# Softmax denominators of an attention block: one group an iteration instead of two, y stored before it is divided, gates kept in DRAM

## The chip, the cores and the metric

The kernel runs on 1 core of a Trainium2 chip. The metric is the device time of one execution in microseconds, the median over several runs. Engines are called by the profile's names: PE (TensorE), DVE (VectorE), ACT (ScalarE), POOL (GpSimd), SP (SyncE, which here only issues DMAs).

## The reference

One transformer block with adaptive layer norm, batch B = 2, sequence S = 2048, width H = 512, 16 heads of 32, all float32:

```
c6 = silu(c) @ Wc + bc
sh_msa, sc_msa, g_msa, sh_mlp, sc_mlp, g_mlp = split(c6, 6)
xm = layernorm(x) * (1 + sc_msa) + sh_msa
q, k, v = xm @ Wq + bq, xm @ Wk + bk, xm @ Wv + bv     # 16 heads of 32
w = softmax(q k^T / 32) ; y = w v
x = x + g_msa * (y @ Wo + bo)
xm2 = layernorm(x) * (1 + sc_mlp) + sh_mlp
x = x + g_mlp * (gelu(xm2 @ W1 + b1) @ W2 + b2)
```

## The kernel before

The program has three stages, `project`, `attend` and `feed_forward`, each a block in which every engine runs its own list of instructions, ordered by semaphores alone. At the end of a stage the engines meet.

**project** computes q, k, v and the modulation vectors for 8 blocks of 512 tokens and stores q, k and v in DRAM. It also computes the gates (g_msa, g_msa*bo, g_mlp, g_mlp*b2 for both batch entries, 8 tiles of 128x512), which stay in SBUF in `sh.gates`, 16 KB of each partition.

**attend** has 32 iterations (`N_IT`): iteration i handles one group of 4 heads and 512 queries against all 2048 keys; four iterations (`BPB`) share a head group. In an iteration there are 16 tiles of 128 keys. For each tile and head PE makes scores (L1221), ACT takes their exponential into `probs` (L1054), a ring of 5 tiles, and PE multiplies with v into `y_bank` (L1232), two tiles at a time. Between these PE makes the scores once more for the maxima of the next iteration (L1205), which DVE reduces (L1078).

The denominators are sums of the exponentials over all keys. They are made so:

- Each group of 4 tiles is a quad c (4 an iteration, `QPI`). POOL adds tiles 0 and 1 of the quad (`first_pair`, L905, two instructions, heads 0-1 and 2-3) and tiles 2 and 3 (`second_pair`, L916, two instructions).
- POOL then issues accumulating DMAs (`accumulate`, L920), 1 MB each: `fold_quad` adds the second sum to the first, `fold_half` adds the first sum of an odd quad to that of the even quad before it. Two quads make a half h, so an iteration has 4 quad folds and 2 half folds.
- PE multiplies each half with a matrix of ones (`sums`, L1238), 4 matmuls of 128x32 on 512 columns, which the profile shows as 8 records; when such a group is due says `due_sums`. ACT copies the result (`take_sum`, L991), a small DMA gathers it (`move_sums`), DVE adds the two halves and inverts (`invert_small`), and two more DMAs store the inverses and load them back broadcast over 128 partitions (`store_inv`, `load_inv`).
- ACT copies y out of PSUM (`take_y`), POOL multiplies it with the inverses two iterations later (`normalise`, L954), and ACT's queue stores it to `y_cols` (`store_y`).

A slot of `probs` is given back to ACT only when its y matmuls and POOL's sum over it are done (`slot_free`); a home of a half sum is given back to POOL when PE's `sums` over it is done (`first_free`); `second_pair(c)` waits for the fold of quad c - 2, `fold_half` for that of the odd quad.

The last iteration differs: its sums aren't folded by DMA, DVE makes some of them, and the first output projection, residual, norm and up product of the next stage are worked in.

**feed_forward** runs over 8 blocks k of 512 tokens. A block has 16 steps j (`MT`): PE makes `up(k, j)` and `down(k, j-1)`, each with three products of rounded high and low parts (lines 1677 to 1679, 12 matmuls each); ACT makes gelu (L1655); DVE rounds and splits h (L1552, L1554) and W1, W2 (L1542, L1547), POOL makes their low parts (L1465, L1470). The attention output of block k + 1 is loaded into `yb`, biased by ACT (`bias_y`), split by DVE (`split_y`, L1505) and multiplied with Wo by PE (`project_out`) at steps 3 to 6; transposes follow at steps 10 to 13. SP's queue loads y, x, and the quarters 1 to 3 of W1 and W2 (`w_raw`). In block 0 the last iteration's y is still to be normalised, by DVE reciprocals (L1612) and by POOL (L1445).

Of the kernel before, what the change touches and what calls it, by code (L numbers as in the profile page):

```python
# [40 lines left out]
HALF_QUADS = 2  # L41
LAST_HALF = LAST_QUAD // HALF_QUADS
HPI = QPI // HALF_QUADS
# [20 lines left out]
class Shared:  # L64


    def __init__(self, nc, ctx):
# [8 lines left out]
        self.gates = sb("gates", [P, B, 4, H])  # L76
# [7 lines left out]
        self.inv_rows = nc.dram_tensor("inv_rows", [HPG, TOK], F32, kind="Internal").ap()  # L84
# [3 lines left out]
class Late:  # L88
# [7 lines left out]
    def __init__(self, nc, ctx):  # L96
# [8 lines left out]
        self.y_buf, self.d_raw, self.inv = sb("y_buf", [P, 2, TOK]), sb("d_raw", [P, HPI, TOK]), sb("inv", [P, TOK])  # L105
        self.d_small, self.d_total = sb("d_small", [P, HPI, HPG * TOK // P]), sb("d_total", [P, HPG * TOK // P])
# [5 lines left out]
        self.y_normed, self.last_normed, self.y_stored = sem("y_normed"), sem("last_normed"), sem("y_stored")  # L112
        self.y_taken, self.d_taken, self.small_ready = sem("y_taken"), sem("d_taken"), sem("small_ready")
        self.inv_stored, self.inv_in = sem("inv_stored"), sem("inv_in")


class Feed:


    def __init__(self, nc, ctx, sh, late):  # L120
# [12 lines left out]
        self.w1_parts = late.space[5].parts  # L133
        self.stats, self.mv = sb("stats2", [P, TT, 6]), sb("mv2", [P, TT, 2])
# [5 lines left out]
        self.y_in, self.x_in = [sem(f"y_in{g}") for g in range(G)], [sem(f"x2_in{q}") for q in range(2)]  # L140
        self.wo_in, self.wo_hi_ready, self.wo_split, self.half_ready = sem("wo_in"), sem("wo_hi_ready"), sem("wo_split"), sem("half_ready")
# [33 lines left out]
def project(nc, sh, late, x, c, Wc, bc, Wq, bq, Wk, bk, Wv, bv, b1, bo, b2):  # L175
# [5 lines left out]
    with ExitStack() as ctx:  # L181
# [15 lines left out]
        c_part = sb("c_part", [P, 2, H])  # L197
        w_raw = [t.plain[:, :, :] for t in sh.space]
# [32 lines left out]
        next_in, ones_early = sem("next_in"), sem("ones_early")  # L231
# [44 lines left out]
        def _(sp):  # L276
# [55 lines left out]
            for k in range(NBLK - 1):  # L332
# [12 lines left out]
            sp.wait_ge(ones_early, BPB)  # L345
            for s in qk_stored:
                sp.wait_ge(s, 1 + 16 * NBLK * N_QK // 4)
# [40 lines left out]
        def _(v):  # L388
# [71 lines left out]
            def gate(e, b):  # L460
# [4 lines left out]
                after(v.tensor_tensor(sh.gates[:, b, gate, :], g_bank[:, :], bc_wide[:, wide, :], ALU.add))  # L465
                v.tensor_tensor(sh.gates[:, b, bias, :], sh.gates[:, b, gate, :], bc_wide[:, 2 + wide, :], ALU.mult).then_inc(g_taken, 1)
# [243 lines left out]
def due_sums(b):  # L710

    if b >= N_BLOCKS - 3:
        first = LAST_HALF + b - (N_BLOCKS - 3)
        return (first - 1, first) if first == LAST_HALF else (first,)
    return ((b - 9) // 4,) if b >= 9 and b % 4 == 1 else ()


class MaxRing:
# [4 lines left out]
    def __init__(self):  # L727
        uses = []
        for i in range(N_IT):
            for s in range(N_SC):  # L730
# [4 lines left out]
                if within == 2 * HPG - 1:  # L735
                    uses += [("sum", u) for u in due_sums(b) if u <= LAST_HALF]
# [10 lines left out]
    def last_banks(self):  # L747

        held = [self.bank["sum", LAST_HALF + n] for n in (-2, -1, 0)]
# [4 lines left out]
def attend(nc, sh, late, feed, x, Wo, W1, W2):  # L754
# [7 lines left out]
    with ExitStack() as ctx:  # L762
# [14 lines left out]
        half_sum = [sb(f"half_sum{n}", [P, HPG, TOK]) for n in range(3)]  # L777
# [3 lines left out]
        y_buf, d_raw, inv = late.y_buf, late.d_raw, late.inv  # L781
        d_small, d_total, inv_small = late.d_small, late.d_total, late.inv_small
# [14 lines left out]
        quad_folded, half_folded = [sem(f"quad_folded{n}") for n in range(2)], sem("half_folded")  # L797
        y_taken, d_taken, y_normed, small_ready = late.y_taken, late.d_taken, late.y_normed, late.small_ready
        d_moved, d_summed = sem("d_moved"), sem("d_summed")
        inv_stored, inv_in, y_stored = late.inv_stored, late.inv_in, late.y_stored  # L800
# [6 lines left out]
        def first_home(c):  # L807
            if c >= LAST_QUAD:
                return (half_sum[2], first_sum[0], first_sum[1], half_sum[2])[c - LAST_QUAD]
# [16 lines left out]
        def _(sp):  # L826
# [46 lines left out]
            for c in range(BPB):  # L873
                load_v(0, c)
# [894 lines left out]
```

## Time and profile before

| | us |
|---|---|
| median of 3 runs (lowest to highest) | 2735.59 (2729.82 to 2737.03) |
| the profiled execution: its time | 2730.14 |
| its span, first to last instruction | 2728.0 |
| PE busy | 2690.0 |
| DVE busy | 2007.5 |
| POOL busy | 1870.5 |
| ACT busy | 1341.3 |

The profiled execution is on the low side of the runs. project ends at about 344 us, attend at about 1923 us. The busy time of PE contains the overlap of pipelined matmuls only once. "DMA share" is the mean busy share of the 16 DMA engines; packets of two queues that overlap on one engine can bring it over 1.

### The profile page before, as it was taken

To read this page: it belongs to the slowest core of one execution; us is meant where nothing else is said; L and a number is where in the kernel's file an instruction comes from. 1 tells how busy PE (TensorE), PEld (TensorE's weight loads), DVE (VectorE), ACT (ScalarE), POOL (GpSimd) and SP (SyncE) were. 2 spreads that over 40 slices of the span, in tenths; PEclk is the share of its full clock that TensorE was granted. 3 is DMA by queue.
4 is the path that set the end of the run, shared out by engine and by line. 5 is a ranking of instruction groups with operands and counts; after the bars stand their busy time and mean duration, and the time that the engine had idled before them with its cause. 6 is when DMAs were issued, how large, how long until landed. Compare 5 with 4: busy or idle time off the path is not lost. (4 is left out here: it accounts for less than half of the span.)

```text
span 2728.0 us, 37942 instructions
## 1 busy us (share of the span) xinstructions
PE 2690.0 (99%) x13737; PEld 1780.1 (65%) x13737; DVE 2007.5 (74%) x3326; ACT 1341.3 (49%) x2534; POOL 1870.5 (69%) x1083
## 2 busy tenths in 40 slices
PE   7999999999999999999999999999999999999998
PEld 5777755555555555555555555554788888888887
DVE  6557688888888888888888888887675765765754
ACT  2322267676676766767667676776221221221211
POOL 1000088989989999998999989897655455555553
PEclk9999999999999999999999999999999999999999
DMA  6555458788888879878888888875410110110000
GB/s 247 204 186 165 159 128 176 167 185 179 178 182 174 187 167 189 182 166 185 178 179 184 174 186 170 198 166 121 147 41 11 47 46 2 47 47 1 31 16 16
DMA packets 143754, 369.22 MB, mean 135 GB/s; under 512 B 23572, under 2 KB 40528, under 8 KB 119760
## 3 DMA queue, kind: packets, MB, share of 16 engines
q0 software_dynamic: 26784, 195.05, 35.8%
q1 hardware_dynamic: 96000, 155.26, 19.0%
q10 hardware_dynamic: 20784, 16.49, 2.1%
q8 instruction: 110, 1.80, 0.3%
q14 instruction: 76, 0.62, 0.1%
HBM read 111.97 MB, written 58.97 MB: 63 GB/s over the span
## 5 line engine op out<-in xcount | busy, mean ns | idle before, releaser
L1078 DVE TENSOR_REDUCE part_max<-shared_bank 128x1 f32<-128x512 f32 x1972 | 1207.3, 680 | 274.2 <-PE shared_bank L1205 274.1
L1054 ACT ACTIVATE probs<-s_bank 128x512 f32<-128x512 f32 x2048 | 1034.3, 627 | 289.0 <-PE s_bank L1221 285.2
L1232 PE MATMUL y_bank<-probs,vs 128*32 128x512 f32 x4096 | 493.2, 599 | 0.0
L905 POOL TENSOR_TENSOR first_sum<-probs 128x1024 f32<-128x1024 f32 x124 | 343.5, 2771 | 78.4 <-ACT probs L1054 78.3
L1655 ACT ACTIVATE h<-shared_bank,vecs 128x512 f32<-128x512 f32 x128 | 88.1, 688 | 562.9 <-PE shared_bank L1679 558.0
L1221 PE MATMUL s_bank<-late_parts 97*128 97x512 f32 x848 | 349.3, 413 | 2.5 <-ACT probs L1054 2.5
L905 POOL TENSOR_TENSOR half_sum<-probs 128x1024 f32<-128x1024 f32 x124 | 336.9, 2733 | 14.7 <-ACT probs L1054 14.6
L1205 PE MATMUL shared_bank<-late_parts 96*128 96x512 f32 x848 | 336.6, 397 | 0.9
L916 POOL TENSOR_TENSOR wo<-probs 128x1024 f32<-128x1024 f32 x124 | 335.0, 3063 | 0.4 <-ACT probs L1054 0.4
L916 POOL TENSOR_TENSOR second_sum<-probs 128x1024 f32<-128x1024 f32 x128 | 317.8, 2625 | 13.4 <-ACT probs L1054 6.4
L1465 POOL TENSOR_TENSOR late_parts<-w_raw,late_parts 128x512 fp32r<-128x512 f32 x96 | 129.2, 1346 | 226.3 <-DVE late_parts L1542 226.3
L1232 PEld LDWEIGHTS y_bank<-probs,vs 128*32 128x32 f32 x4096 | 106.9, 109 | 241.4 <-issue 121.7
L1221 PEld LDWEIGHTS s_bank<-late_parts 97*128 97x128 f32 x848 | 160.0, 189 | 133.5 <-issue 88.0
L1552 DVE CAST h_hi<-h 128x512 fp32r<-128x512 f32 x128 | 79.7, 623 | 179.2 <-ACT h L1655 179.1
L1677 PE MATMUL acc_bank<-w_hi,h_hi 128*128 128x512 f32 x512 | 201.4, 393 | 1.4 <-DVE h_lo L1554 1.3
L1677 PE MATMUL shared_bank<-late_parts 128*128 128x512 f32 x508 | 201.2, 396 | 1.1 <-PEq L762 1.1
L1679 PE MATMUL acc_bank<-w_hi,h_lo 128*128 128x512 f32 x512 | 200.8, 392 | 0.0
L1679 PE MATMUL shared_bank<-late_parts 128*128 128x512 f32 x508 | 199.3, 392 | 0.0
L1678 PE MATMUL acc_bank<-w_lo,h_hi 128*128 128x512 f32 x512 | 199.0, 389 | 0.0
L1678 PE MATMUL shared_bank<-late_parts 128*128 128x512 f32 x508 | 198.8, 391 | 0.0
L1205 PEld LDWEIGHTS shared_bank<-late_parts 96*128 96x128 f32 x848 | 161.4, 190 | 30.5 <-DVE part_max L1078 5.4
L1221 PE MATMUL s_bank<-space_parts,late_parts 97*128 97x512 f32 x432 | 177.7, 412 | 0.0
(199 smaller groups left out, 4566.8 us busy)
## 6 DMA issues: line engine op xcount, KB each, us to landing
half_sum<-second_sum POOLq DMA_DIRECT2D x62, 1024.0 KB, 13.5
first_sum<-wo POOLq DMA_DIRECT2D x62, 1024.0 KB, 10.0
half_sum<-first_sum POOLq DMA_DIRECT2D x62, 1024.0 KB, 7.6
late_plain<-in_x SPq DMA_DIRECT2D x16, 1024.0 KB, 7.0
q_parts<-qk_out SPq DMA_DIRECT2D x32, 512.0 KB, 3.1
k_parts<-qk_out SPq DMA_DIRECT2D x32, 512.0 KB, 3.4
late_parts<-q_parts SPq DMA_DIRECT2D x63, 256.0 KB, 11.4
late_parts<-k_parts SPq DMA_DIRECT2D x60, 256.0 KB, 11.8
```

The source lines that it names most:

```text
L905: pool.tensor_tensor(first_home(c)[:, hs, :], probs[:, 4 * c % RING, hs, :], probs[:, (4 * c + 1) % RING, hs, :], ALU.add).then_inc(first_ ...
L916: pool.tensor_tensor(second_home(c)[:, hs, :], probs[:, (4 * c + 2) % RING, hs, :], probs[:, (4 * c + 3) % RING, hs, :], ALU.add).then_inc ...
L1054: act.activation(probs[:, tile % RING, h, :], s_bank[(HPG * tile + h) % 3][:, :], ACT.Exp).then_inc(p_done, 1)
L1078: v.tensor_reduce(part_max[:, i % 2, hs, c:c + 1], m_bank[ring.bank["max", i, n]][:, :], AX.X, ALU.max).then_inc(m_taken, 1)
L1205: pe.matmul(m_bank[ring.bank["max", i, n]][:, :], queries[i % 3][0:STACK, h, s * P:(s + 1) * P], keys[u][0:STACK, h, :], start=True, stop= ...
L1221: pe.matmul(s_bank[n % 3][:, :], keys[u][0:STACK + 1, h, s * P:(s + 1) * P], queries[i % 3][0:STACK + 1, h, :], start=True, stop=True).the ...
L1232: last = pe.matmul(y_bank[h * DH:(h + 1) * DH, :], vs[:, t, h * DH:(h + 1) * DH], probs[:, tile % RING, h, :], start=(t == 0), stop=(t == ...
L1465: pool.tensor_tensor(feed.w1_lo(j), w1_raw[j * 4 // MT][:, :, j % (MT // 4) * P:(j % (MT // 4) + 1) * P], feed.w1_hi(j).bitcast(F32), ALU. ...
L1655: act.activation(h[:, j % 2, :], up_bank[j % 2][:, :], ACT.Gelu, bias=sh.vecs[:, ROW_B1 + j:ROW_B1 + j + 1]).then_inc(up_taken, 1)
L1677: pe.matmul(bank, hi_l, hi_r, start=first, stop=False)
L1678: pe.matmul(bank, hi_l, lo_r, start=False, stop=False)
L1679: return pe.matmul(bank, lo_l, hi_r, start=False, stop=last)
```

## The change

Four things are changed together.

1. **One denominator group an iteration.** A new accumulating DMA, `fold_whole(i)`, adds the second half sum of an iteration to the first; POOL issues it in the third quad of the next iteration. PE's `sums` is then done once an iteration instead of twice (the last two iterations keep halves and pairs). There are 5 homes for half sums instead of 3, 16 KB more of each partition. `take_sum`, `move_sums` and `invert_small` are done once, without the addition.
2. **y stored as it comes.** For 28 of 32 iterations `store_y` stores y straight after `take_y`, undivided; `normalise` and `load_inv` remain for the first block of each of the first four head groups (iterations 0, 4, 8, 12), whose y the last iterations of attend need. All inverses go to a DRAM tensor with a row for each iteration.
3. **Division in feed_forward.** `load_y` loads the inverses broadcast (4 more DMAs of 256 KB) beside y; POOL multiplies (`scale_y`, 4 instructions of 128x512 a block), in the last four steps of the block before; for block 1 in steps 1 and 2 of block 0. There everything for block 1 is shifted by two steps (`later`): bias at step 3, split at 4, output projection at 5 to 8, transposes at 12 to 15. The reciprocals of 128x512 in block 0 are gone.
4. **Gates in DRAM.** `project` stores all gates (2 MB) from SP's queue; attend loads two of the tiles (512 KB), feed_forward the other six (1.5 MB) behind the second quarters of W1 and W2.

```diff
+        self.gate_rows = nc.dram_tensor("gate_rows", [P, B * 4, H], F32, kind="Internal").ap()
-        self.inv_rows = nc.dram_tensor("inv_rows", [HPG, TOK], F32, kind="Internal").ap()
+        self.inv_rows = nc.dram_tensor("inv_rows", [N_IT, HPG, TOK], F32, kind="Internal").ap()
...
+def in_first_block(i):
+    return i < G * BPB and i % BPB == 0
+def plain_before(i):
+    return i - min((i + BPB - 1) // BPB, G)
...
                     load_early(qm[1], sh.q_parts, Q_PARTS, 1, qm_early[1])
+                    sp.dma_start(sh.gate_rows, gates[:, :, :]).then_inc(gates_stored, 16)
...
-    return ((b - 9) // 4,) if b >= 9 and b % 4 == 1 else ()
+    return ((b - 17) // 8,) if b >= 17 and b % 8 == 1 else ()
...
-            return half_sum[c // 2 % 3] if c % 2 == 0 else first_sum[c // 2 % 2]
+            return half_sum[c // 2 % HALVES] if c % 2 == 0 else first_sum[c // 2 % 2]
...
+            sp.dma_start(feed.first_gates[:, :, :], sh.gate_rows[:, 0:2, :]).then_inc(feed.gates_in, 16)
             for i in range(N_IT - 1):
                 iteration(i)
...
-                if c % 2 == 0 and h >= 3:
-                    pool.wait_ge(d_done, h - 2)
+                if c % 2 == 0 and h >= HALVES:
+                    old = h - HALVES
+                    if old % 2 == 0:
+                        pool.wait_ge(d_done, old // 2 + 1)
+                    else:
+                        pool.wait_ge(whole_folded, 16 * (old // 2 + 1))
...
+            def fold_whole(i):
+                pool.wait_ge(half_folded, 16 * (2 * i + 2))
+                accumulate(half_sum[2 * i % HALVES][:, :, :], half_sum[(2 * i + 1) % HALVES][:, :, :]).then_inc(whole_folded, 16)
...
-                if c % QPI == QPI - 2 and c // QPI >= 2:
-                    normalise(c // QPI - 2)
+                if c % QPI == QPI - 2 and 1 <= c // QPI < LAST:
+                    fold_whole(c // QPI - 1)
+                if c % QPI == QPI - 2 and c // QPI >= 3 and in_first_block(c // QPI - 3):
+                    normalise(c // QPI - 3)
...
-                    if tile >= 20 and tile % 8 == 4 and (tile - 20) // 8 < LAST_HALF:
-                        take_sum((tile - 20) // 8)
+                    if t == 4 and i >= 2:
+                        take_sum(i - 2)
...
+                    if i and t == 5 and not in_first_block(i - 1):
+                        store_y(i - 1)
...
-                if u < LAST_HALF:
-                    pe.wait_ge(half_folded, 16 * (u + 1))
+                if u < LAST - 1:
+                    pe.wait_ge(whole_folded, 16 * (u + 1))
                     for h in range(HPG):
-                        last = add_up(u, h, first_home(2 * u)[:, h, :], True, True)
+                        last = add_up(u, h, half_sum[2 * u % HALVES][:, h, :], True, True)
+                elif u == LAST - 1:
+                    pe.wait_ge(half_folded, 16 * (2 * u + 2))
+                    for h in range(HPG):
+                        add_up(u, h, half_sum[2 * u % HALVES][:, h, :], True, False)
+                        last = add_up(u, h, half_sum[(2 * u + 1) % HALVES][:, h, :], False, True)
...
+        def later(k):
+            return 2 if k == 0 else 0
...
                 for g in range(G):
+                    rows = sh.inv_rows[BPB * (group + g) + k % BPB]
                     sp.dma_start(yb[:, g, :], sh.y_cols[group + g, :, tok:tok + TOK]).then_inc(y_in[g], 16)
+                    sp.dma_start(inv[:, g, :], rows.rearrange("h (a n) -> h a n", a=1).broadcast_to([HPG, DH, TOK])).then_inc(inv_in[g], 16)
...
             load_w1(1)
             load_w2(1)
-            sp.wait_ge(late.inv_stored, 16 * (N_IT - 1))
-            sp.dma_start(late.inv[:, :], sh.inv_rows.rearrange("h (a n) -> h a n", a=1).broadcast_to([HPG, DH, TOK])).then_inc(late.inv_in, 16)
+            sp.dma_start(gates[:, :, :], sh.gate_rows[:, 2:4 * B, :]).then_inc(gates_in, 16)
+            sp.wait_ge(late.y_taken, N_IT)
+            sp.wait_ge(late.y_stored, 16 * plain_before(LAST))
+            sp.dma_start(sh.y_cols[LAST // BPB, :, LAST % BPB * TOK:(LAST % BPB + 1) * TOK], late.y_buf[:, :]).then_inc(late.y_stored, 16)
+            sp.wait_ge(late.d_taken, N_IT)
+            sp.dma_start(late.d_small[:, :], late.d_raw[0:P:DH, :]).then_inc(late.d_moved, 16)
...
+            def scale_y(k, g):
+                pool.wait_ge(y_in[g], 16 * (k + 1))
+                pool.wait_ge(inv_in[g], 16 * k)
+                pool.tensor_tensor(yb[:, g, :], yb[:, g, :], inv[:, g, :], ALU.mult).then_inc(y_scaled, 1)
...
+                    if k == 0 and j in (1, 2):
+                        scale_y(1, 2 * j - 2)
+                        scale_y(1, 2 * j - 1)
...
+                    if k + 2 < NBLK and j >= MT - G:
+                        scale_y(k + 2, j - (MT - G))
...
-                    if has_next and j == (1 if k == 0 else 0):
+                    if has_next and j == (3 if k == 0 else 0):
                         bias_y(k + 1)
```

## Rows read from the trace of the kernel before

**Rows 1.** The page's busy times: engine, busy us, share of the span, instructions.

```profile
PE 2690.0 (99%) x13737; PEld 1780.1 (65%) x13737; DVE 2007.5 (74%) x3326; ACT 1341.3 (49%) x2534; POOL 1870.5 (69%) x1083
```

**Rows 2.** Stretches by stage: length, busy us by engine, granted clock, DMA share, GB/s.

```profile
0.00:341.00 341.00, 322.76 (x1442) 253.32 (x1442) 208.38 (x398) 91.63 (x137) 21.45 (x25) 1.00 0.56 192
...
380.00:1600.00 1220.00, 1217.50 (x6829) 685.19 (x6827) 995.80 (x1707) 846.07 (x1680) 1104.59 (x575) 1.00 0.84 178
...
1923.00:2728.00 805.00, 794.94 (x3508) 647.61 (x3508) 519.94 (x782) 159.53 (x241) 436.10 (x322) 1.00 0.11 38
```

**Rows 3.** PE's timeline in attend: start us, us, line, operands, count.

```profile
1210.68 1.92 PE L1232 MATMUL y_bank<-probs,vs 128*32 128x512 f32 x16
1212.42 1.04 PE L1238 MATMUL shared_bank<-half_sum,ones 128*32 128x512 f32 x8
...
1217.35 1.92 PE L1232 MATMUL y_bank<-probs,vs 128*32 128x512 f32 x16
1223.14 1.92 PE L1232 MATMUL y_bank<-probs,vs 128*32 128x512 f32 x16
```

**Rows 4.** Groups with shapes apart: count, busy us, mean ns, idle before and releaser.

```profile
L920 POOL DMA_DIRECT2D half_sum<-first_sum x62 | 57.9, 934 | 27.2 <-DMA first_sum<-wo 27.2
L954 POOL TENSOR_TENSOR y_buf<-y_buf,inv 128x512 f32<-128x512 f32 x30 | 55.8, 1861 | 5.0 <-ACT probs L1054 5.0
L1537 DVE TENSOR_TENSOR late_parts<-late_plain,late_parts 128x512 fp32r<-128x512 f32 x28 | 17.4, 684 | 0.0
```

**Rows 5.** POOL's timeline in attend, brackets: idle before and releaser.

```profile
1206.76 1.45 POOL L920 DMA_DIRECT2D first_sum<-wo  x1
...
1209.72 2.13 POOL L954 TENSOR_TENSOR y_buf<-y_buf,inv 128x512 f32<-128x512 f32 x1
...
1241.26 2.38 POOL L905 TENSOR_TENSOR first_sum<-probs 128x1024 f32<-128x1024 f32 x1 [0.87 <-ACT probs L1054]
1245.63 0.87 POOL L920 DMA_DIRECT2D half_sum<-first_sum  x1 [2.00 <-DMA first_sum<-wo]
...
1246.78 3.01 POOL L905 TENSOR_TENSOR first_sum<-probs 128x1024 f32<-128x1024 f32 x1
```

**Rows 6.** Stretches inside attend, columns as in rows 2.

```profile
1214.00:1218.00 4.00, 4.00 (x23) 2.70 (x25) 3.83 (x7) 4.00 (x9) 3.31 (x3) 1.00 0.00 0
...
1224.40:1249.20 24.80, 24.80 (x145) 13.80 (x138) 20.23 (x35) 17.08 (x34) 20.27 (x12) 1.00 1.02 215
1163.00:1357.80 194.80, 194.40 (x1100) 109.39 (x1092) 158.72 (x273) 135.11 (x268) 177.25 (x93) 1.00 0.85 180
```

**Rows 7.** DMA queues: packets, MB, share of 16 engines over the span; q0 is POOL's.

```profile
q0 software_dynamic: 26784, 195.05, 35.8%
...
q10 hardware_dynamic: 20784, 16.49, 2.1%
```

**Rows 8.** SP's queue at the start of feed_forward, timeline.

```profile
1923.06 1.77 SPq L1388 DMA_DIRECT2D yb<-y_cols  x4
...
1925.90 0.59 SPq L1391 DMA_DIRECT2D w_raw<-in_L_cond_W  x1
```

**Rows 9.** DVE, ACT and PE in block 0, timelines.

```profile
1935.45 0.43 DVE L1542 CAST late_parts<-w_raw 128x512 fp32r<-128x512 f32 x1 [0.28 <-DMA w_raw<-in_L_cond_W]
...
1936.13 6.88 DVE L1505 TENSOR_TENSOR y_lo<-yb,y_hi 128x512 fp32r<-128x512 f32 x4
...
1937.70 0.69 ACT L1655 ACTIVATE h<-shared_bank,vecs 128x512 f32<-128x512 f32 x1 [4.82 <-PE shared_bank L1679]
...
1943.06 0.50 PE L1677 MATMUL shared_bank<-space_parts,y_hi 128*128 128x512 f32 x1 [0.55 <-DVE y_lo L1505]
```

**Rows 10.** The chain of waits where block 1 begins: start us, us, what.

```profile
2028.30 4.61 DVE late_plain L1565 x4
...
2033.28 0.70 DVE h_lo L1554
2034.12 0.47 PE acc_bank L1677
```

More of the change, by code:

```diff
@@ L747, in last_banks @@
     def last_banks(self):
-        held = [self.bank["sum", LAST_HALF + n] for n in (-2, -1, 0)]
+        held = [self.bank["sum", LAST + n] for n in (-2, -1, 0)]
         unused, = set(range(self.BANKS)) - set(held)
@@ L982, in take_y @@
                 act.wait_ge(av_done, NKT * (i + 1))
-                if i >= 2:
-                    act.wait_ge(y_stored, 16 * (i - 1))
-                act.activation(y_buf[:, i % 2, :], y_bank[:, :], ACT.Copy).then_inc(y_taken, 1)
-            def take_sum(h):
-                act.wait_ge(d_done, h + 1)
-                if h >= HPI and h % HPI == 0:
-                    act.wait_ge(d_moved, 16 * h)
-                act.activation(d_raw[:, h % HPI, :], m_bank[ring.bank["sum", h]][:, :], ACT.Copy).then_inc(d_taken, 1)
+                if in_first_block(i):
+                    if i:
+                        act.wait_ge(first_y_stored, 16 * (i // BPB))
+                    act.activation(first_y_buf[:, :], y_bank[:, :], ACT.Copy).then_inc(y_taken, 1)
+                else:
+                    if plain_before(i):
+                        act.wait_ge(y_stored, 16 * plain_before(i))
+                    act.activation(y_buf[:, :], y_bank[:, :], ACT.Copy).then_inc(y_taken, 1)
@@ L993, in take_last_sums, with take_sum @@
+            def take_sum(i):
+                act.wait_ge(d_done, i + 1)
+                if i:
+                    act.wait_ge(d_moved, 16 * i)
+                act.activation(d_raw[:, :], m_bank[ring.bank["sum", i]][:, :], ACT.Copy).then_inc(d_taken, 1)
             def take_last_sums():
-                act.wait_ge(d_done, LAST_HALF + QPI)
-                act.wait_ge(d_moved, 16 * LAST_HALF)
-                act.activation(d_raw[:, 0, :], m_bank[ring.bank["sum", LAST_HALF]][:, :], ACT.Copy).then_inc(d_taken, 1)
+                act.wait_ge(d_done, LAST + QPI)
+                act.wait_ge(d_moved, 16 * LAST)
+                act.activation(d_raw[:, :], m_bank[ring.bank["sum", LAST]][:, :], ACT.Copy).then_inc(d_taken, 1)
@@ L1358, in feed_forward @@
         gated = sb("gated", [P, TT, TOK])
+        inv = sb("inv_wide", [P, KT, TOK])
+        gates = sb("gates2", [P, B * 4 - 2, H])
+        gates_in, inv_in, y_scaled = sem("gates2_in"), [sem(f"inv2_in{g}") for g in range(G)], sem("y_scaled")
         acc_bank = [pb(f"acc_bank{t}", [P, H]) for t in range(TT)]
```

232 lines of the change are left out of this document (117 added, 115 removed).

## The prediction

> **What bounds the kernel now.** I read the page's busy times first, and the reader is to see that one engine stands out: PE is busy 2690.0 of 2728.0 us, the others at most 74% [rows 1]. A share over a whole span can hide stages with other limits, so next come the windows by stage. In the steady part of attend PE is busy 1217.50 of 1220 us, in feed_forward 794.94 of 805 us, and the clock is granted in full in both [rows 2]. So in attend a microsecond taken from PE's list is a microsecond off the end, as long as nothing else becomes late. What is near to becoming late is seen in the same row: POOL is busy 1104.59 of 1220 us (91%), DVE 82%, ACT 69%, and the DMA engines show a share of 0.84 [rows 2]. The change takes from PE and gives to DMA, so these two are read closely below. In feed_forward the DMA share is 0.11 and POOL is at 54% [rows 2], but single steps are tight there: at the start a weight quarter lands just when DVE wants it, and PE waits 0.55 us for the split of y [rows 9].
>
> **Part 1, the sums on PE.** PE's timeline shows the price. From one pair of y products to the next takes 1217.35 - 1210.68 = 6.67 us where a sum stands between, and 1223.14 - 1217.35 = 5.79 us where none does [rows 3], so a group costs 0.88 us; its own record of 1.04 us overlaps its neighbours. An iteration lasts 48.7 us (four of them in 194.8 us [rows 6]). Before there are 62 groups of halves; after there are 30 of wholes and one with two parts for iteration 30, the work of 32. The pairs of the last iteration stay. 30 groups x 0.88 us = **-26.4 us**, all on the engine that sets the pace.
>
> **Part 1, the extra fold.** Two things pay for it, POOL's time and the DMA engines' time.
>
> POOL: the record of an issue has 0.87 us and more, but between 1245.63 and the add at 1246.78 there are two issues (half and quad) [rows 5], so one costs POOL 0.6 us of its list. At the same place in its list it loses the multiplication of y, 1.86 us by its mean [rows 4], in 26 of 30 cases. POOL's list becomes shorter by about 1 us an iteration (1.86 x 26 / 30 - 0.6), which about matches the 0.88 us that the iteration becomes shorter. Nothing from POOL, then, if it does not wait more for DMAs.
>
> DMA: the folds took 35.8% of 2728 us for 186 MB-sized transfers [rows 7], which is 976.6 / 186 = 5.25 us of all 16 engines each. The four iterations of rows 6 show a share of 0.85, so 0.85 x 48.7 = 41.4 us an iteration. Added are 5.25; taken away is about half of the ACT queue's q10, which had 2.1% of 2728 us [rows 7], 1.8 us an iteration, so 0.8 us. The sum is 45.8 us in an iteration of 47.82 us: a share of 0.96. It fits, and not by much. Where it is put matters. `fold_whole` is issued where `normalise` was, at 1209.7 us in the trace [rows 5], behind the fold of the odd quad issued at 1206.76. That one is through at 1214, and from 1214 to 1218 the DMA engines stood at 0.00 [rows 6]. So the new transfer fills 4 us of a hole and runs about 1.3 us into the next two folds. From 1224.4 to 1249.2 the share is 1.02 [rows 6], key and query loads beside folds, so those 1.3 us are handed on, less the 1 us or so of broadcast inverses that no longer runs there.
>
> What is late next is the wait at 1245.63, where POOL stood 2.00 us for the odd quad's fold [rows 5]; over the kernel such waits sum to 27.2 us in front of half folds [rows 4]. Behind it in POOL's list is the second half of `first_pair`, which ends at 1246.78 + 3.01 = 1249.8 us. Its slot of the ring is wanted by ACT four tiles later. ACT released the first half at 1241.26 [rows 5], half a tile after it began the tile, with 48.7 / 16 = 3.04 us a tile: it began at about 1239.9, and wants the slot at 1252.0. The slack is 2.2 us, and I expect 0.3 to 1.3 us of it to be used. Cost: **0**, bounds 0 and 1.5 us in each of 30 iterations (45 us) should the fold come 3.7 us later. I take the lower end since the hole is there in the trace.
>
> The Trainium skill (DMA: Bandwidth & Descriptors, section "Issuing engines are not separate DMA queues") speaks against the change: transfers from POOL, SP and ACT run on the same 16 engines and interleave. The row that bears on it is the share of 1.02 while loads and folds meet, and by that the trace agrees. The page's 6.15 us for 1 MB from DRAM would make 46.7 us of demand an iteration, an estimate from its table, still under 47.82.
>
> **Part 1, the rest.** ACT loses one `take_sum` and one gather an iteration, DVE a small addition; neither sets the pace. PE's sum over a whole comes some 8 tiles after its fold is issued (third quad of the next iteration to tile 3 of the one after), 24 us; freeing homes later is covered by five of them. Cost 0.
>
> **Part 2 and 3 in steady feed_forward.** Four instructions of 128x512 a block are added to POOL, 1.3 to 1.9 us each (1.86 in attend [rows 4]), against 46% of idle time there. They stand in steps 12 to 15, when y and inverses have been loaded for long. One of them runs beside DVE's results at the block's end, which are on the chain (4.61 us for four [rows 10]). Cost 0, bounds 0 and 1 us in six blocks.
>
> **Part 3 in block 0.** Here there is no cover. Two effects:
>
> (a) SP issues 8 loads instead of 4 ahead of x and W1's second quarter. Four took 1.77 us, so the quarter's issue moves from 1925.90 to about 1928 us [rows 8], and 1 MB of inverses runs ahead of it. It landed at 1935.45 and DVE had to wait 0.28 us for it [rows 9]. It now lands between +2 us (issue alone) and +6 us (issue and a further 1 MB). PE wants the part made of it for `up(0, 4)`. gelu(3) began at 1937.70 [rows 9] as `up(0, 3)` ended; then PE has the 12 matmuls of `down(0, 2)`, at 794.94 / 3508 = 0.23 us each [rows 2] 2.7 us, and no output projection now, so it wants the part at 1940.4. DVE's 0.43 us [rows 9] and POOL's 1.3 to 1.9 lie between: landing must be at 1938.1 to 1938.7, that is about +3 us. Stall: 0 to 3.3 us, I take 0.5.
>
> (b) POOL does two multiplications in each of steps 1 and 2, waits behind them for DVE's parts, and by my count has the fourth done about 1945 us. ACT's bias then delays gelu(4) by some 3 us, which PE's two-step lead swallows, but DVE's split of y (6.88 us for four [rows 9]) begins only 2 us ahead of PE's projection instead of 4.4: PE waits about 2 us instead of 0.55. **+1.5 us**, bounds 0 and 5.
>
> The Trainium skill (GPSIMD Engine Reference, section "8. Key points") says that POOL and DVE contend when a DVE instruction has two SBUF inputs. The trace has 1.72 us each for y's split beside POOL's work and 0.684 us for an instruction of the same shape beside an idle POOL, so it agrees. At 0.684 us each (b) would be about 0.
>
> (c) Transposes two steps later end right before the last `down` of block 0. At about 0.7 us for each instruction of this shape (0.684 [rows 4], 0.69 [rows 9]) the last modulation, four roundings and the last split end 4.2 us after them, and two weight casts follow, 0.4 us each; DVE's gated results, which used to begin as `down` ended, 2.7 us after, begin at 5.0. DVE is some 2 us late into block 1, where PE met DVE's h_lo with no slack [rows 10]. I take **+1 us**, bounds 0 and 3.
>
> **Part 4.** 2 MB stored at about 303 us, where the stage's DMA share is 0.56 [rows 2], 5 to 10 us of it, and four q and k stores may be outstanding; 512 KB at attend's start; 1.5 MB in feed_forward ahead of a use at step 5 (about 1951 us, landing by about 1948). Each is hidden by that room; without it some 3 us. Cost 0, bounds 0 and 3.
>
> **Sum.** -26.4 + 0.5 + 1.5 + 1 = -23.4 us. The profiled execution took 2730.14 us with a span of 2728.0; after it I expect a span of 2704.6 and a time of 2706.7, a factor of 0.9914. The median of the runs lay 5.45 us above that execution, and 0.9914 x 2735.6 = **2712 us**.
>
> **Rivals.**
>
> 1. *As forecast*: the sums are gone, small stalls in block 0. 2712 us, 2706 to 2719. Chance 0.66.
> 2. *Block 0 pays more*: quarter 1 of W1 lands 6 us late, then W2's, with POOL blocked behind its multiplications. For it: the 0.28 us wait shows no slack. Against: the next wants are each a step apart. All upper bounds of block 0 (3.3 + 5 + 3) and half of part 4's: 2735.6 - 26.4 + 12.8 = 2722 us. Chance 0.14.
> 3. *The DMA engines or POOL become the pace, in part*: each iteration loses about what the sum gave, 0.8 us. For it: a share of 0.96, POOL at 91%. It begins where the odd quad's fold lands over 2.2 us later than now. 2735.6 - 23.4 + 30 x 0.8 = 2736 us, no measurable change. Chance 0.09.
> 4. *The same place, in full, slower*: the fold lands 3.7 us later in each iteration, ACT waits 1.5 us for its slot and PE for ACT. 2735.6 - 23.4 + 45 = 2757 us. Against it: 4 us of idle DMA where the transfer is put, and heavy loads in three of four iterations only. Chance 0.07.
> 5. *The saved sums don't shorten the interval*, because PE now waits for ACT or DVE instead. Against: both are well under PE. 2736 us, chance 0.04.
>
> A change of 0.3% (8 us) is about what a measurement of this kernel can tell from none. Cases 1 and 2 are faster (0.80). Cases 3 and 5 are the same, but for 0.02 in which case 3 costs a little more (0.11); with that and case 4, slower has 0.09. The range must leave out no more than two in ten: 2703 (full gain and the lower of the runs) to 2731.
>
> **What would show it.** In the changed profile: 8 PE records fewer per iteration at the sums' line and an interval of 47.8 us between `neg_max_row` loads; 0.00 share windows in attend gone, a share near 0.96; POOL's waits for `first_sum` folds up from 27 us but under 60; ACT still with almost no wait for POOL in attend; in block 0 PE waits of 2 to 4 us in all. It would be wrong if ACT's waits for POOL's sums reach tens of us, if PE shows waits in attend, or if PE's waits for DVE in blocks 1 to 6 exceed a microsecond each.

## The result, and the profile after

| | before | after |
|---|---|---|
| median of 5 runs (lowest to highest), us | 2735.5 (2729.82 to 2737.03) | 2724.47 (2721.32 to 2727.01) |
| ratio after/before, 95% interval | | 0.9963 (0.9948 to 0.9977) |
| the profiled execution: time, span | 2730.14, 2728.0 | 2725.18, 2723.1 |

The kernel became faster by 0.37%, some 10 us. Forecast was 0.86%, 23.5 us. The sign and the place of the gain were as forecast; more than half of the forecast gain was lost again. The two profiled executions are only 4.9 us apart, since that of before lay 5 us under its kernel's median and that of after 1 us over its own; the table below is of these two, and single executions of one kernel differ by some us.

Where, is read best by cutting both spans at four events that both kernels have: the 2nd and the 32nd load of `neg_max_row` on SP's queue, at 333.8 us the first (30 iterations lie between the two), PE's first instruction of feed_forward, and DVE's first gated result of blocks 0 and 7. The cuts in the before were at 385.86, 1844.56, 1923.25, 2023.01 and 2720.17 us, in the after at 384.97, 1818.03, 1900.63, 2016.00 and 2715.22.

| stretch, us | before | after | difference | forecast |
|---|---|---|---|---|
| up to the 2nd load | 385.86 | 384.97 | -0.9 | 0 |
| 30 iterations | 1458.70 | 1433.06 | -25.6 | -26.4 |
| 32nd load to the start of feed_forward | 78.69 | 82.60 | +3.9 | 0 |
| block 0 | 99.76 | 115.37 | **+15.6** | **+3** |
| blocks 1 to 7 | 697.16 | 699.22 | +2.1 | 0 |
| rest | 7.83 | 7.88 | 0 | 0 |

Busy times and queues of the page after, to be set beside [rows 1] and [rows 7]:

```profile
PE 2674.8 (98%) x13497; PEld 1776.7 (65%) x13497; DVE 1997.7 (73%) x3291; ACT 1326.0 (49%) x2503; POOL 1902.4 (70%) x1114
...
q0 software_dynamic: 31104, 226.51, 41.6%
...
q10 hardware_dynamic: 13404, 9.68, 1.3%
```

PE has 240 instructions fewer, 8 for each of the 30 groups. Its busy time fell by 25.1 us in the 30 iterations, but by 15.2 us in all: it rose by 4.4 us in the last iteration and by 4.7 us in block 0, in both of which part of the work ran at the lower clock. q0 carries 30 MB-sized folds more.

**Attend.** Three neighbouring `neg_max_row` loads of after, from SP's queue: the interval is 47.9 us, was 48.7.

```profile
1196.75 0.51 SPq L856 DMA_DIRECT2D space_parts<-neg_max_row  x1
1244.64 0.51 SPq L856 DMA_DIRECT2D late_parts<-neg_max_row  x1
1292.49 0.52 SPq L856 DMA_DIRECT2D late_parts<-neg_max_row  x1
```

Four of these iterations, in a window with the columns of [rows 2]: PE without a gap, a DMA share of 0.97. The two folds' groups stand below it, to be set beside [rows 4]: POOL's wait in front of the half folds went from 27.2 to 25.6 us, and the new fold has none.

```profile
1000.00:1191.50 191.50, 191.09 (x1061) 108.70 (x1060) 158.06 (x268) 133.16 (x264) 177.27 (x94) 1.00 0.97 202
```

```profile
L945 POOL DMA_DIRECT2D half_sum<-first_sum x62 | 62.1, 1002 | 25.6 <-DMA first_sum<-wo 25.6
L945 POOL DMA_DIRECT2D half_sum<-half_sum x30 | 43.7, 1458 | 0.0
```

**Block 0.** PE's waits over the whole kernel, and the windows around the first of them (columns as in [rows 2]):

```profile
PE shared_bank L1733 <- POOL late_parts L1527: 10.2, 1, 10.2
...
PE acc_bank L1733 <- DVE h_lo L1619: 2.3, 4, 1.4
```

```profile
1905.00:1910.00 5.00, 5.00 (x23) 4.11 (x22) 3.12 (x4) 0.45 (x1) 4.03 (x4) 1.00 0.63 173
1910.00:1915.00 5.00, 5.00 (x23) 4.05 (x23) 2.21 (x2) 0.24 (x1) 3.67 (x3) 1.00 0.99 261
...
1920.00:1925.00 5.00, 0.00 (x0) 0.00 (x0) 0.00 (x0) 0.00 (x0) 0.00 (x0) 0.54 1.05 408
1925.00:1930.00 5.00, 2.03 (x5) 1.65 (x6) 0.76 (x2) 0.00 (x0) 3.46 (x3) 0.50 0.81 299
1930.00:1935.00 5.00, 3.65 (x10) 2.38 (x9) 1.56 (x5) 3.26 (x5) 1.62 (x2) 0.60 0.95 324
```

PE stands still from 1917.8 to 1927.97, and from 1920 to 1925 no compute engine works. When it starts again the granted clock is 0.50, the lower of its two levels (1.2 GHz). The twelve matmuls that follow come 0.43 us apart; at the full clock they come 0.23 us apart. That is another 12 x 0.20 = 2.4 us. Waits of 10.2 and 1.4 and the clock's 2.4 make 14.0 of the 15.6 us.

What PE waits for is behind POOL's part: DVE waits for the weight quarter, and behind that, on DVE, for the last denominators. SP's queue at the stage's start shows when the quarter (`w_raw`) was issued:

```profile
1900.49 0.34 SPq L1449 DMA_DIRECT2D yb<-y_cols  x1
...
1905.46 0.94 SPq L1450 DMA_DIRECT2D inv_wide<-inv_rows  x1
1906.44 2.65 SPq L1459 DMA_DIRECT2D late_plain<-in_x  x1
1909.14 2.51 SPq L1461 DMA_DIRECT2D inv_rows<-inv_small  x1
1911.69 0.73 SPq L1453 DMA_DIRECT2D w_raw<-in_L_cond_W  x1
1912.46 3.72 SPq L1456 DMA_DIRECT2D w_raw<-in_L_cond_W  x1
...
1920.73 0.66 SPq L1469 DMA_DIRECT2D d_small<-d_raw  x1
```

```profile
1926.04 0.43 DVE L1607 CAST late_parts<-w_raw 128x512 fp32r<-128x512 f32 x1 [13.51 <-DMA w_raw<-in_L_cond_W]
...
1933.41 0.25 DVE L1674 RECIPROCAL inv_small<-d_small 128x16 f32<-128x16 f32 x1 [6.61 <-DMA d_small<-d_raw]
```

The quarter was issued 11.20 us after the first load of y. In [rows 8] it was 2.84 us. It landed 25.5 us after that load, before 12.4 us [rows 8, 9]. SP's own issue records became long: 2.5 to 3.7 us for three of them, where at the same place before they took 0.3 to 0.6 us. Each of the two waits above is one of DVE's, in its list order, so everything else that DVE has to do is behind it.

The time of the landing hides a second thing. The trace holds every event in which a DMA's semaphore rises. For these loads they came as follows:

| load | issued | events of its semaphore |
|---|---|---|
| W1's quarter, before | 1925.90 | 16 from 1933.88 to 1935.43 |
| W1's quarter, after | 1911.69 | 12 from 1918.62 to 1919.13, 4 from 1924.85 to 1926.01 |
| the fourth inverse load, after | 1905.46 | 1 at 1906.83, 4 from 1919.17 to 1920.87 |
| gather of the last denominators, after | 1920.73 | 1 at 1921.81, 4 from 1932.27 to 1933.38 |

Twelve of the quarter's sixteen parts were there 18.6 us after the first load of y, and the other four 6.9 us later. An inverse load reads four DRAM rows, the gather four partitions, and both end with four late events. That fits loads which four of the 16 DMA engines carry alone, so that on these four everything behind them is late; which engine moved a packet isn't in the trace, so this is inferred. The kernel before has one load of this kind in feed_forward, of 256 KB, issued at 1932.92. Its events were 1 at 1933.98 and 4 from 1940.86 to 1943.14, 10.2 us after the issue.

### The profile page after: what moved, and what is told of

Read it like the earlier page. It is cut to its first block and busy times, and to the rows that moved or that the text cites. A ratio compares the mean times of both kernels' runs of the same rounds, so it can differ in the third digit from the quotient of the medians.

```text
span 2723.1 us, 37337 instructions
## 1 busy us (share of the span) xinstructions
PE 2674.8 (98%) x13497; PEld 1776.7 (65%) x13497; DVE 1997.7 (73%) x3291; ACT 1326.0 (49%) x2503; POOL 1902.4 (70%) x1114
## 5 line engine op out<-in xcount | busy, mean ns | idle before, releaser
L926 POOL TENSOR_TENSOR first_sum<-probs 128x1024 f32<-128x1024 f32 x124 | 350.9, 2832 | 63.4 <-ACT probs L1094 63.4
L926 POOL TENSOR_TENSOR half_sum<-probs 128x1024 f32<-128x1024 f32 x124 | 335.5, 2714 | 15.3 <-ACT probs L1094 15.2
L941 POOL TENSOR_TENSOR second_sum<-probs 128x1024 f32<-128x1024 f32 x126 | 324.2, 2805 | 9.7 <-ACT probs L1094 6.0
L1617 DVE CAST h_hi<-h 128x512 fp32r<-128x512 f32 x128 | 91.0, 711 | 177.9 <-ACT h L1711 177.8
L1733 PE MATMUL shared_bank<-late_parts 128*128 128x512 f32 x508 | 202.0, 398 | 11.3 <-POOL late_parts L1527 10.2
## 6 DMA issues: line engine op xcount, KB each, us to landing
half_sum<-second_sum POOLq DMA_DIRECT2D x62, 1024.0 KB, 13.2
half_sum<-half_sum POOLq DMA_DIRECT2D x30, 1024.0 KB, 10.4
```

What stands on the lines that cost most here:

```text
L926: pool.tensor_tensor(first_home(c)[:, hs, :], probs[:, 4 * c % RING, hs, :], probs[:, (4 * c + 1) % RING, hs, :], ALU.add).then_inc(first_ ...
L941: pool.tensor_tensor(second_home(c)[:, hs, :], probs[:, (4 * c + 2) % RING, hs, :], probs[:, (4 * c + 3) % RING, hs, :], ALU.add).then_inc ...
L1617: v.tensor_copy(h_hi[:, j % 2, :], h[:, j % 2, :]).then_inc(h_hi_step, 1)
L1733: pe.matmul(bank, hi_l, hi_r, start=first, stop=False)
```

## The experiments

Each kernel's stretches, cut as above, of its profiled execution, with the median and the ratio to the kernel before, which ran on the same chip (us; a stretch is of one execution each, so 1 us between two of them means little):

| kernel | median | ratio | 30 iterations | last iteration | block 0 | blocks 1-7 |
|---|---|---|---|---|---|---|
| before | | 1 | 1458.70 | 78.69 | 99.76 | 697.16 |
| after | 2724.47 | 0.9963 | 1433.06 | 82.60 | 115.37 | 699.22 |
| after_again | 2721.73 | 0.997 | 1431.21 | 79.95 | 116.39 | 699.10 |
| two_halves | 2746.41 | 1.0055 | 1457.21 | 76.91 | 117.60 | 699.14 |
| w1_first | 2724.11 | 0.9976 | 1431.56 | 82.69 | 116.90 | 698.94 |
| invert_late | 2720.0 | 0.9959 | 1431.35 | 80.03 | 112.76 | 698.97 |
| both | 2711.8 | 0.993 | 1431.15 | 80.43 | 105.65 | 698.78 |
| late_no_inverses | 2707.21 | 0.9914 | 1432.49 | 80.07 | 100.95 | 698.76 |
| no_steady_scale | 2713.01 | 0.9934 | 1432.43 | 81.69 | 105.88 | 697.83 |
| fold_busy | 2811.36 | 1.031 | 1523.99 | 83.57 | 105.93 | 699.08 |
| fold_twice | 2828.7 | 1.035 | 1542.81 | 81.59 | 105.93 | 699.06 |
| extra_load | 2761.38 | 1.01 | 1489.06 | 80.97 | 105.22 | 699.01 |

two_halves, w1_first, invert_late and both ran on one chip (before there: 2731.02), late_no_inverses, fold_busy, fold_twice and no_steady_scale on another (2730.65), extra_load and after_again on a third (2730.01).

**two_halves**: everything of the change but the one group an iteration.

```diff
-                if c % QPI == QPI - 2 and 1 <= c // QPI < LAST:
-                    fold_whole(c // QPI - 1)
...
-                if u < LAST - 1:
-                    pe.wait_ge(whole_folded, 16 * (u + 1))
-                    for h in range(HPG):
-                        last = add_up(u, h, half_sum[2 * u % HALVES][:, h, :], True, True)
-                elif u == LAST - 1:
+                if u < LAST:
                     pe.wait_ge(half_folded, 16 * (2 * u + 2))
```

> The changed kernel, but PE again multiplies both half sums with ones (8 matmuls of 128x32 for an iteration instead of 4) and the third kind of fold is left out; everything else stays. If the saved group on PE is what made attend shorter, with 0.85 us each, the interval between neg_max_row loads goes back from 47.9 to 48.7 us and the time rises by 30 x 0.85 = 25 us to about 2750 us. Rival: attend became shorter because POOL and the ACT queue were relieved of the division of y; then the interval stays near 47.9 us, or falls since 30 MB of folds are gone, and the time stays near 2724 us.

The 30 iterations took 1457.21 us, 24.2 more than after (26.0 more than after_again): 0.80 to 0.87 us for a group. By the ratios it is (1.0055 - 0.9963) x 2731 = 25 us, 0.84 each. The gap in the timeline had said 0.88 [rows 3]. The saved sums are the whole gain but for 1.5 us of the iterations, and the rest of the change alone makes the kernel slower by 0.55% (interval 1.0042 to 1.0069).

**w1_first**: the second quarter of W1 goes to the head of SP's queue, that of W2 behind y and the inverses.

```diff
+            load_w1(1)
             load_y(1)
+            load_w2(1)
             sp.dma_start(xb[1][:, :, :], x_blocks[1]).then_inc(x_in[1], 16)
...
-            load_w1(1)
-            load_w2(1)
```

> The changed kernel, but at the start of feed_forward SP issues quarter 1 of W1 ahead of y and the inverses, and quarter 1 of W2 right behind them. Theory A (the quarter lands late because of its place in the queue): DVE's wait of 13.5 us for w_raw goes, but DVE then meets the gathered last denominators, which land some 33 us into the stage, so its wait of 6.6 us grows instead; gain 0 to 6 us, 2718 to 2724 us. Rival B (the 2.5 MB more that are moved there are what costs, in any order): no change in the time of block 0, and y becomes late instead.

The wait for the weights was gone, and nothing was gained: block 0 took 116.90 us. DVE's reciprocal of the last denominators (`invert_last`, at step 2) now had the wait, and PE stood 13.8 us behind it.

```profile
1930.86 0.25 DVE L1674 RECIPROCAL inv_small<-d_small 128x16 f32<-128x16 f32 x1 [19.78 <-DMA d_small<-d_raw]
```

**invert_late**: this reciprocal at step 9 instead.

```diff
-                    if k == 0 and j == 2:
+                    if k == 0 and j == 9:
                         invert_last()
```

> The changed kernel, but DVE inverts the last denominators at step 9 of block 0 instead of step 2. Theory A: the wait of 6.6 us for the gather is gone, the one of 13.5 us for the weights stays; PE's stall of block 0 shrinks by some 4 us: 2720 us. Rival B (the weights and the clock alone cost): no change, 2724 us.

Block 0 became 2.6 us shorter than in after, 3.6 than in after_again. The wait for the quarter stayed.

```profile
1923.22 0.43 DVE L1607 CAST late_parts<-w_raw 128x512 fp32r<-128x512 f32 x1 [13.35 <-DMA w_raw<-in_L_cond_W]
```

**both**: the two edits together.

> The changed kernel with both edits, W1's quarter first and the inversion at step 9. Theory A: neither wait is left, block 0 takes 93 to 97 us from PE's first instruction to the gated results instead of 108.6 counted from its start, and the time is 2709 to 2713 us, that is 12 to 15 us less than the changed kernel and 24 us less than before. Rival B: still 2720 us or more, with PE waiting for y.

Block 0 fell to 105.65 us, and the ratio to 0.993 (0.9917 to 0.9942): the fastest version with all of the work, 19 us under the before. So there were two waits in a row for the same late queue, each hiding the other. The time was as expected, but block 0 wasn't (93 to 97 us expected): DVE still waited 7.5 us for W2's quarter, of which twelve parts had landed by 1914.91 and four by 1923.67, and PE 3.0 us behind it. Removing either alone gave -1.5 to 2.6 us of block 0, both together gave 9.7.

**late_no_inverses**: `invert_late`, and feed_forward loads no inverses; POOL multiplies y with itself instead. The division is left out for all blocks but the first.

```diff
-                    sp.dma_start(inv[:, g, :], rows.rearrange(...).broadcast_to([HPG, DH, TOK])).then_inc(inv_in[g], 16)
...
-                pool.tensor_tensor(yb[:, g, :], yb[:, g, :], inv[:, g, :], ALU.mult)
+                pool.tensor_tensor(yb[:, g, :], yb[:, g, :], yb[:, g, :], ALU.mult)
```

> The run with the inversion at step 9 and the queue in the changed kernel's order, but the inverses are not loaded in feed_forward and POOL multiplies y with itself, so y is left undivided by its sums. Theory A1 (the four broadcast loads are what delays quarter 1 of W1): PE's stall of 10.0 us for its part falls under 3 us and the time from 2720 to about 2709 us. Theory A2 (the rest of the queue, gates and all, delays it): the stall stays above 7 us, 2717 to 2720 us.

Against `invert_late` 11.8 us of block 0 are gone, with the order of the queue and POOL's multiplications unchanged. SP's queue and DVE's first weight cast:

```profile
1898.92 1.77 SPq L1449 DMA_DIRECT2D yb<-y_cols  x4
1900.73 0.43 SPq L1458 DMA_DIRECT2D late_plain<-in_x  x1
...
1901.75 0.74 SPq L1452 DMA_DIRECT2D w_raw<-in_L_cond_W  x1
```

```profile
1911.13 0.76 DVE L1605 CAST late_parts<-w_raw 128x512 fp32r<-128x512 f32 x1 [0.42 <-DMA w_raw<-in_L_cond_W]
```

And a window of it (columns as in [rows 2]): 394 GB/s, where the after with its broadcast inverses in flight moved 173 and 261 GB/s.

```profile
1905.00:1910.00 5.00, 5.00 (x23) 4.05 (x23) 2.81 (x5) 0.69 (x1) 4.04 (x4) 1.00 1.06 394
```

It is the four inverse loads that hold up the queue and the engines, not the multiplications. 1 MB of plain loads at 394 GB/s would be 2.7 us, so their bytes alone are not the reason either. Without them the 16 events of W1's quarter lie between 1909.64 and 1911.10 again, with no four behind. What in these loads does it, the broadcast or that they read only four rows, no run tells apart; the gather, which broadcasts nothing and moves 8 KB, shows the same four late events, which speaks for the four rows. The same 1 MB arranged in more rows wasn't run.

**fold_busy**: `both`, with the new fold issued one quad (12 us) later, where key loads and folds meet.

```diff
-                if c % QPI == QPI - 2 and 1 <= c // QPI < LAST:
+                if c % QPI == QPI - 1 and 1 <= c // QPI < LAST:
                     fold_whole(c // QPI - 1)
```

> The version with both edits of block 0 (2711.8 us), but the new fold is issued one quad later, in the quad that already has a half fold and a quad fold and where the key and query loads run. Theory H (the transfer costs nothing only because it fills a hole): POOL's waits for folds of odd quads rise from 26 us to over 60 us, ACT waits for POOL, and the interval rises from 47.9 us to 48.5 or more: 2725 us or more. Rival S (there is slack for it anywhere): waits rise, but ACT and PE don't notice: 2712 us.

It was slower by 3.8% than `both`, by neither of the mechanisms expected. The DMA share fell to 0.89, so the DMA engines were not the pace. PE itself waited, for the fold that it is about to multiply with ones; its waits over the kernel, and one of the 30:

```profile
PE shared_bank L1287 <- DMA half_sum<-half_sum: 65.9, 30, 3.4
PE s_bank L1270 <- ACT probs L1094: 12.3, 5, 11.4
```

```profile
1059.97 1.93 PE L1287 MATMUL shared_bank<-half_sum,ones 128*32 128x512 f32 x8 [2.20 <-DMA half_sum<-half_sum]
```

PE's place for the sum is fixed. In after the fold is issued at 1194.67 and PE's sum over it begins at 1220.75, a cover of 26 us; 12 were taken away. In after it lands 10.4 us after its issue in the median, here, beside more traffic, 15.7 us, so that what was left was too little. The waits are 2.2 us each, the iterations became 3.1 us longer in the mean. Of the 93 us in all, 66 are these waits. PE waited another 11.4 us at one place, near the end of attend, for ACT, which itself waited 13.2 us for the load of Wo (`space_plain`). And some 34 us of the iterations ran at the lower clock, none of `both`'s, which at half the pace is up to 17 us (an estimate).

**fold_twice**: `both`, with the new fold done a second time behind the first, one quad later; the second half counts twice in the denominators.

> The version with both edits (2711.8 us), but the new fold is done twice, in the third and in the fourth quad, so that the odd half is counted twice in the sums. Its purpose is to find the DMA engines' limit: demand by the shares of the trace is 45.8 + 5.25 = 51 us of all engines in an iteration of 47.9. If shares add up as in the prediction, DMA becomes the pace: interval about 51 us, time about 2800 us. If a share near 1 still hides room, the interval stays under 48.5 us and the time under 2730 us.

```profile
PE shared_bank L1290 <- DMA half_sum<-half_sum: 69.9, 30, 4.0
```

The same wait, so this kernel says nothing of the DMA engines that fold_busy had not said: PE must wait for the second fold. It was a badly chosen test of the share.

**extra_load**: a cleaner one. `both`, and SP copies 1 MB more an iteration from DRAM to DRAM.

```diff
                 load_row(i + 1)
+                sp.dma_start(sh.spare[i], sh.v_rows[0:TOK, :].rearrange("(p a) n -> p (a n)", p=P)).then_inc(late.spare_done, 16)
```

> The version with both changes in block 0 (W1's quarter first, last inverses late), and in attend SP's queue copies 1 MB more a iteration from DRAM to DRAM into a tensor that nobody reads or waits for (31 times), issued behind the load of the maxima's row. It asks for nothing but time of the DMA engines. Theory A (a share of 0.97 means full): 0.97 x 47.9 us is 46.5 us of demand, and a fold, the nearest row, takes 5.25 us, together 51.7 us in an interval of 47.9. So PE, ACT or POOL come to wait for folds or keys, the interval grows to about 51 or 52 us and the time by 90 to 120 us. Theory B (a share of 0.97 is an engine that has a packet open, not one that has no room, since 202 GB/s flow where 400 flowed in feed_forward): the interval stays within 0.3 us of 47.9, the time within 10 us of 2712.

An iteration grew from 47.71 to 49.64 us in the mean, 1.01 in the ratio (1.0073 to 1.0126) against 0.993: +47 us, between the two theories. (The profiled execution is the slowest of four, 2749 to 2771 us.) The price of the copy can be read from the queues of the two pages, `both` first:

```profile
q1 hardware_dynamic: 100128, 166.28, 20.4%
```

```profile
q1 hardware_dynamic: 101120, 198.79, 23.9%
```

23.9% of 2768.5 less 20.4% of 2710.4 us is 108.8 us for 31 copies, 3.5 us each, not a fold's 5.25. `both` has a share of 0.96 in the same window as above, 46.0 us an iteration; 46.0 + 3.5 = 49.5, and 49.64 were measured. That the two agree is partly luck, since the growth isn't even. The intervals between `neg_max_row` loads stay at 47.8 us in 11 of the 30 iterations and reach 51 to 54 us in 9. One takes 62.3 us, where PE waits 11.2 us for ACT and ACT 12.9 us for the load of Wo. Of the 58 us by which this profile is longer than that of `both`, 38 are PE's waits for ACT:

```profile
PE s_bank L1273 <- ACT probs L1097: 38.3, 26, 11.2
```

And 41 us of the iterations ran at the lower clock, which is up to 20 us by the same estimate as above. What is shown is that a share of 0.96 left too little room for a copy of 3.5 us: over the 30 iterations the share rose from 0.95 to 0.98, the new folds landed in 15.5 us instead of 10.2, and PE came to wait behind them. Theory B is refuted; of theory A the direction holds and neither its price for the copy nor an even pace. The wait that grew, POOL's for the fold two quads back, was 3.7 us in after:

```profile
L944 POOL TENSOR_TENSOR second_sum<-probs 128x1024 f32<-128x1024 f32 x126 | 322.9, 2781 | 104.8 <-DMA half_sum<-second_sum 84.3
```

**no_steady_scale**: `both`, without the multiplication of y for blocks 2 to 7 (left undivided).

```diff
                     if k + 2 < NBLK and j >= MT - G:
-                        scale_y(k + 2, j - (MT - G))
+                        g = j - (MT - G)
+                        pool.wait_ge(y_in[g], 16 * (k + 3))
+                        pool.wait_ge(inv_in[g], 16 * (k + 2))
+                        pool.sem_inc(y_scaled, 1)
```

> The version with both edits (2711.8 us), but POOL does not multiply y with the inverses for blocks 2 to 7; the loads remain, and these blocks' y is left undivided. In the changed kernel blocks 1 to 6 took 101.7 us each where they took 101.45 before. If POOL's multiplications beside DVE's work are the cause, the blocks go back to 101.45 us and the time falls by 1 to 1.5 us, to about 2710.5 us. If the loads are the cause, nothing changes.

0.9934 (0.9922 to 0.9947) against 0.993: no change in time that can be measured. Blocks 1 to 7 took 697.83 us, where the other ten kernels with these multiplications took 698.76 to 699.22. So they may carry about 1 us of the 2.

**after_again**: the changed kernel once more, unedited.

> The changed kernel itself, once more, beside the kernel before and the copy kernel on one chip. If its block 0 of about 115 us and the last iteration of attend of about 82 us are its own, they come back within 1 us and 2 us, and the ratio is 0.996 to 0.997. If the last iteration's 4 us over before are the clock's doing in one execution, it comes out near 80 us or below, as in two of the other kernels.

Block 0 came back with 116.39 us, blocks 1 to 7 with 699.10. The last iteration of attend had 79.95, not 82.60; over the kernels with the change's work there it lies between 76.9 and 83.6, and no edit explains which.

## Why the forecast was too good

- **Part 1, the sums on PE** (-26.4 forecast): right. -25.6 and -27.5 us in two executions of after, 24.2 and 25 by undoing it. The gap between y products was a good price.
- **Part 1, the extra fold** (0, up to 45): right, and for the reason given. The forecast share of 0.96 was 0.97. POOL's wait for `first_sum` folds, expected to rise above 27 us, stayed at its place and size (25.6), and ACT waited for POOL nowhere in attend for long enough to be listed. What the working had only in passing was the more delicate thing: it gave PE's sum 24 us of cover (26 in the profile after) and called that enough. fold_busy shows that with 14 us of it PE waits in every iteration, and the kernel is 3.1% slower than before. Rival 3 (the DMA engines or POOL as the pace) did not come about, but extra_load shows how near it was: by the share some 1.4 us an iteration were left (3% of 47.8), and 3.5 us more of demand made the mean iteration 1.9 us longer.
- **Part 3, block 0 (a)**: this is the step that failed. "It now lands between +2 us (issue alone) and +6 us (issue and a further 1 MB)", with a stall of 0.5 us taken, was mis-sized: it landed +13 us, and PE stood 10.2 us. The working priced an inverse load like a y load, by bytes and by an issue time of 0.44 us. But y loads are plain, and the inverse loads broadcast each of four rows over 32 partitions; without them block 0 is 11.8 us shorter (late_no_inverses). Twelve of the quarter's sixteen parts landed at +6.3 us, near the upper bound, though SP issued it 8.4 us later and not 2. The last four came 6.9 us after them, and the working had no term for that. The trace of before had a row for it: its own inverse load took 10.2 us for 256 KB, and from 1937.5 to 1941 us 258 GB/s flowed at a share of 1.06. The rest of the step was right: a landing over +3 us comes through in full, 13 - 3 = 10, and PE's wait was 10.2 us.
- **Block 0, a wait that was not named**: the change gathers the last denominators by a DMA on SP's queue, behind all these loads, where before DVE inverted them directly and no DMA was needed, and DVE waits for it at step 2. The forecast listed DVE's work in this block, but not this wait, nor that h, the weights and y's split are queued behind it. 6.6 us of DVE's time in after, 19.8 in w1_first; worth 2.6 us alone and 11.3 us once the weights are early (116.90 against 105.65).
- **Block 0 (b)**: y's split began at 1939.07, 4 us after PE's second wait had ended, and no wait of PE is put down to it. **(c)**: not told apart from the rest. Both sizes were lost under (a). In `both`, where little of (a) is left, PE waited 1.0 us for y's split.
- **The clock**: not in the forecast at all. 2.4 us of block 0, and a part of the last iteration.
- **Part 4, the gates** (0): not tested by itself. Its 1.5 MB are issued behind both second quarters, but ahead of the gather, so it can have a share in the second wait.
- **The last iteration** (+3.9 and +1.3): the execution with 82.60 us had a granted clock of 0.79 between 1860 and 1890 us (0.92 over the stretch, 0.98 in before and in after_again), and after_again came 2.7 us lower. 1 to 2 us may be the change's, which is not settled.
- **Blocks 1 to 7** (+2, forecast 0 with a bound of 6): half of it goes with the multiplications, by one execution; the other half stays open.

So rival 2 named the right place, "block 0 pays more", at 12.8 us of bounds. The bounds were too low, since that of (a) was taken from loads unlike the ones that were added. That its 2722 us lie within 3 us of the measured 2724.47 is luck: block 0 cost 15.6 us in the profile and not 11.3, some 6 us more were lost outside it, and before's profiled execution was on the low side by 5 us.

## What to carry to other kernels

A transfer is not priced by its bytes alone: a load of another shape, of which no row shows several under load, has an unknown price, and is kept out of the queue in which a stage's first loads stand, or put behind them. A load from four rows was such a shape here. Where the weights wait behind it, see whether all parts of them land together. Where one wait stalls a stage, list every other wait on the same engine that depends on the same queue: undoing one may show nothing because the next takes over, and only both together show what they cost. Where work is moved from an engine to a DMA, keep the distance from its issue to the use that waits for it: 26 us were enough here for a transfer that landed in 10, and 14 were not, when in its new place it landed in 16.

## What the runs showed of the hardware

- Four loads of 256 KB that broadcast four DRAM rows each over 32 partitions, between plain loads, brought the moved data down to 145 to 281 GB/s at shares of 0.57 to 1.09 (windows of 5 us from 1905 to 1920 in after and `both`); without them it was 385 to 417 GB/s at 1.02 to 1.06 (late_no_inverses, 1905 to 1925). A share of 1 does not mean the same rate. One of these windows in `both`, and one of the kernel before, in which its only such load was just issued (at 1932.92):

```profile
1915.00:1920.00 5.00, 5.00 (x23) 4.06 (x22) 1.23 (x2) 2.17 (x4) 1.63 (x2) 1.00 1.09 281
```

```profile
1930.00:1935.00 5.00, 5.00 (x24) 4.08 (x23) 2.83 (x5) 2.57 (x5) 4.09 (x3) 1.00 1.05 399
```

- The semaphore of a plain load of 1 MB rose in 16 events within 1.6 us (before). Behind loads from four rows, which show four late events, twelve of the 16 came together and four 6 to 9 us later (after, `both`).
- An issue on SP takes 0.3 to 0.6 us at the start of a stage and up to 5.9 us behind several MB of loads. In late_no_inverses the ones of over 2 us (up to 5.88) came only with the third and fourth weight quarters; with the inverse loads they began with the load of x (after) or the fourth group of y (`both`). That SP waits for room in its queue is what the pattern suggests; no run measured it by itself.
- PE stood 10.15 us. The granted clock in that window was 0.54, then 0.50, and PE's next twelve matmuls ran at the 1.2 GHz level. The cost of the stall was a quarter more than the wait that the profile shows (2.4 us on 10.2).
- A DRAM to DRAM copy of 1 MB took 3.5 us of all 16 engines. An accumulating fold of 1 MB in SBUF took 5.25 us.
